# The causal mask of attention b added by VectorE inside the row-maximum operation, instead of by TensorE

## The reference

```
K = jnp.einsum('bpd,ihd->biph', x, W_K)
Q = jnp.einsum('bpd,ihd->biph', x, W_Q)
V = jnp.einsum('bpd,ihd->biph', x, W_V)
scores = jnp.einsum('biph,biqh->biqp', K, Q)
mask = jnp.tril(jnp.ones((q_len, q_len), dtype=bool))
scores = jnp.where(mask[None, None, :, :], scores, NEG_INF)
attn = jax.nn.softmax(scores / np.sqrt(d_head).astype(np.float32), axis=-1)
z = jnp.einsum('biph,biqp->biqh', V, attn)
z_flat = jnp.transpose(z, (0, 2, 1, 3)).reshape(b, q_len, -1)
out = jnp.einsum('bqf,df->bqd', z_flat, W_O)
```

## Time and profile before

| | |
|---|---|
| median of 3 executions | 586.08 us (585.6 to 588.6) |
| the profiled execution's own time | 586.4 us, of which the profile's span is 584.6 us |
| TensorE (matmul) busy | 461.3 us, 79% of the span |
| VectorE busy | 380.9 us, 65% |
| ScalarE busy | 225.5 us, 39% |
| GpSimd busy | 239.2 us, 41% |
| share of the chain that ended last | PE 64%, DVE 12%, POOL 9%, DMA 6% |
| row maxima (L1280), all instructions | 128, 62.4 us busy |

### The profile page before, as it was taken

How to read it: one execution, slowest core, us unless ns; L and a number is a source line. 1 busy time by engine, 2 the same in 40 slices (tenths; PEclk the granted TensorE clock), 3 DMA queues, 4 the chain that set the end, 5 groups by cost and what they waited for, 6 DMA issues and landing times.

```text
span 584.6 us, 10870 instructions
## 1 busy us (share of the span) xinstructions
PE 461.3 (79%) x3458; PEld 363.6 (62%) x3458; DVE 380.9 (65%) x1097; ACT 225.5 (39%) x815; POOL 239.2 (41%) x249
## 2 busy tenths in 40 slices
PE   2955694706997099999999999999999964609993
PEld 1422363606996067787877778787777854508993
DVE  6999986843665467767576765757676527825662
ACT  1600001402443046646355554645555333304441
POOL 6202784571544224434343343434334423562543
PEclk9967998556999599999999999999999987558998
DMA  8999500025472200000000000000000000126560
GB/s 293 413 421 422 213 1 1 28 105 167 106 226 72 72 2 2 1 2 1 0 0 0 0 0 0 0 0 0 0 0 0 1 2 1 55 93 185 156 196 20
DMA packets 22003, 47.57 MB, mean 81 GB/s; under 512 B 3248, under 2 KB 13622, under 8 KB 19536
## 3 DMA queue, kind: packets, MB, share of 16 engines
q1 hardware_dynamic: 18960, 40.79, 20.2%
q0 software_dynamic: 3008, 6.34, 3.1%
HBM read 23.88 MB, written 24.15 MB: 82 GB/s over the span
## 4 chain that ended last, share of the span: by engine, by line
PE 64%; DVE 12%; POOL 9%; DMA 6%; issue 5%; ACT 2%; SPq 0%; POOLq 0%; ACTq 0%; DVEq 0%
PE ps L836 10%; PE ps L865 8%; PE ps L904 8%; PE ps L891 7%; PE ps L791 6%; PE ps L853 5%; PE ps L804 5%; PE ps L843 5%; POOL sum L440 3%; DMA pv<-in_w 3%; PE ps L871 3%; POOL sorted_in L464 3%; PE ps L645 2%; POOL sum L444 2%; DVE prod L981 2%
## 5 line engine op out<-in xcount | busy, mean ns | idle before, releaser
L499 POOL TENSOR_TENSOR vT<-vT,prec 128x256 f32<-128x256 f32 (+1 forms) x128 | 103.0, 825 | 168.3 <-DVE prec L1288 168.3
L606 ACT ACTIVATE vT<-ps,nmax 128x128 f32<-128x128 f32 (+1 forms) x256 | 105.1, 435 | 26.1 <-DVE nmax L1280 26.1
L614 ACT COPY prod<-ps 128x384 f32<-128x384 f32 x96 | 42.9, 481 | 117.6 <-PE ps L891 114.2
L1280 DVE TENSOR_REDUCE nmax<-ps 128x2 f32<-128x256 f32 (+1 forms) x128 | 62.4, 550 | 33.9 <-PE ps L871 33.9
L836 PE MATMUL ps<-xnT,wb 128*128 128x256 f32 x256 | 67.0, 385 | 4.6 <-DVE xnT L1260 3.9
L891 PEld LDWEIGHTS ps<-cst,vT 128*128 128x128 f32 x384 | 44.7, 141 | 18.7 <-issue 15.8
L606 ACT ACTIVATION_READ_ACCUMULATOR vT<-ps,nmax 128x1 f32 x256 | 56.1, 219 | 0.0
L891 PE MATMUL ps<-cst,vT 128*128 128x128 f32 x384 | 52.5, 273 | 1.8 <-POOL vT L499 1.7
L904 PE MATMUL ps<-prod 128*64 128x256 f32 (+1 forms) x512 | 49.6, 336 | 3.0 <-ACT prod L614 2.1
L865 PE MATMUL ps<-qk 64*128 64x128 f32 (+1 forms) x512 | 51.0, 338 | 0.0
L836 PEld LDWEIGHTS ps<-xnT,wb 128*128 128x128 f32 x256 | 44.3, 193 | 10.5 <-DVE xnT L1260 4.3
(11 more groups left out here) (148 smaller groups left out, 832.4 us busy)
## 6 DMA issues: line engine op xcount, KB each, us to landing
sorted_in<-zero SPq DMA_DIRECT2D x1, 16512.0 KB, 58.6
pv<-in_w SPq DMA_DIRECT2D x30, 259.0 KB, 3.1
pv<-sorted_in SPq DMA_DIRECT2D x46, 129.0 KB, 2.6
wps<-in_w SPq DMA_DIRECT2D x1, 2072.0 KB, 9.2
w2s<-in_w SPq DMA_DIRECT2D x1, 2048.0 KB, 13.9
wb<-in_w_b SPq DMA_DIRECT2D x1, 1536.0 KB, 18.0
xres<-in_x SPq DMA_DIRECT2D x4, 256.0 KB, 4.0
xres<-after_ffn SPq DMA_DIRECT2D x4, 256.0 KB, 3.8
```

The costliest lines, as they stand in the source:

```text
L499: last = nc.gpsimd.tensor_tensor(px, px, view(prec, m_at(n, x) + t * 2, [[1, 2], [0, (t + 1) * P]]), ALU.mult)
L606: last = nc.scalar.activation(pb[:, o:o + (t + 1) * P], wide[:, c:c + (t + 1) * P], ACT.Exp, bias=nmax[:, m:m + 1], accum_out=psum[:, m:m ...
L614: nc.scalar.copy(pT[:, c:c + BLOCKS * P], bank[hh][:, 0:BLOCKS * P]).then_inc(b_pa, 1)
L1280: last = nc.vector.tensor_reduce(nmax[:, m:m + 2], view(wide, x * 1024 + t * P, [[512, 2], [1, (t + 1) * P]]), AX.X, ALU.max, negate=True)
```

## The change

The mask matmuls go, with their two bfloat16 tiles and the casts that filled them. `max_b` becomes eight tensor_tensor_reduce operations a step, one for each head and tile. Each reads the scores from PSUM and the mask from SBUF, writes minus their sum back over the scores in PSUM, and gives the minimum of what it wrote, which is minus the row maximum, through the accumulator. For tile 1 the mask row is 128 zero columns (new, at `C_OPEN` of the constants) followed by the causal block. The exponential takes scale -1. `b_s` is now raised once a step, after the scores of both pairs, and VectorE waits for it ahead of `invert(n, 1)`.

```
@@ -62,7 +62,7 @@
 SKIP = 4096.0
 
 
-C_ID, C_BEFORE, C_CAUSAL, C_FIRST, C_UPTO = 0, 128, 256, 384, 392
+C_ID, C_BEFORE, C_OPEN, C_CAUSAL, C_FIRST, C_UPTO = 0, 128, 256, 384, 512, 520
 C_SLOT = C_UPTO + NE * NE
 C_NEXT = C_SLOT + NDYN
 C_FULL = C_NEXT + NDYN
@@ -241,8 +241,6 @@
 
         wb = sb("wb", [P, 3 * HB * DHB])
         wob = sb("wob", [P, NPAIR * D])
-        id_bf = sb("id_bf", [P, P], BF16)
-        causal = sb("causal", [P, P], BF16)
         qk = sb("qk", [P, RING * 2 * L])
         nmax = sb("nmax", [P, 2 * 2 * 2 * T])
         psum = sb("psum", [P, 2 * 2 * 2 * T])
@@ -604,7 +602,7 @@
                         o, m = p_at(n, x, hh, t), m_at(n, x) + t * 2 + hh
                         c = (2 * x + hh) * 512 + t * P
                         last = nc.scalar.activation(pb[:, o:o + (t + 1) * P], wide[:, c:c + (t + 1) * P], ACT.Exp,
-                                                    bias=nmax[:, m:m + 1], accum_out=psum[:, m:m + 1])
+                                                    bias=nmax[:, m:m + 1], scale=-1.0, accum_out=psum[:, m:m + 1])
                 last.then_inc(b_e, 1)
 
             def copy_p(n, x, hh):
@@ -862,16 +860,11 @@
                     for hh in range(2):
                         rows = slice(hh * DHB, (hh + 1) * DHB)
                         c = (2 * x + hh) * 512 + t * P
-                        nc.tensor.matmul(wide[:, c:c + (t + 1) * P], qk[rows, r + t * P:r + (t + 1) * P],
-                                         qk[rows, r + L:r + L + (t + 1) * P],
-                                         start=t == 0, stop=False, skip_group_check=True)
-
-            def mask_b(x):
-                for hh in range(2):
-                    last = nc.tensor.matmul(view(wide, (2 * x + hh) * 512, [[2 * P, 2], [1, P]]), id_bf[:],
-                                            view(causal, 0, [[0, 2], [1, P]]), start=False, stop=True,
-                                            skip_group_check=True)
-                last.then_inc(b_s, 1)
+                        last = nc.tensor.matmul(wide[:, c:c + (t + 1) * P], qk[rows, r + t * P:r + (t + 1) * P],
+                                                qk[rows, r + L:r + L + (t + 1) * P],
+                                                start=t == 0, stop=t == T - 1, skip_group_check=True)
+                if x == 1:
+                    last.then_inc(b_s, 1)
 
             def turn_p(n, x):
                 pe.wait_ge(b_n, 2 * nth(n) + x + 1)
@@ -912,11 +905,8 @@
                 if ok(n1):
                     scores_b(n1, 0)
                     scores_b(n1, 1)
-                    mask_b(0)
                 if ok(n):
                     turn_p(n, 0)
-                if ok(n1):
-                    mask_b(1)
                 if ok(n2):
                     project_qk(n2, 0)
                 if some(bv) and j != 1 or some(b) and j == 1:
@@ -1045,9 +1035,7 @@
                 norm_a(u)
             dve.wait_ge(in_c, 16)
             nc.vector.tensor_copy(before[:], cst[:, C_BEFORE:C_BEFORE + P])
-            nc.vector.tensor_copy(id_bf[:], ident)
-            nc.vector.tensor_copy(region[:], cst[0:1, C_REGION:C_REGION + GT * NE])
-            nc.vector.tensor_copy(causal[:], cst[:, C_CAUSAL:C_CAUSAL + P]).then_inc(in_r, 1)
+            nc.vector.tensor_copy(region[:], cst[0:1, C_REGION:C_REGION + GT * NE]).then_inc(in_r, 1)
             for c in range(4):
                 products(0, c)
             products(1, 0)
@@ -1273,13 +1261,18 @@
                 dve.wait_ge(b_t, 4 * nth(n) + 4)
                 nc.vector.tensor_copy(pT[:, 2 * BLOCKS * P:3 * BLOCKS * P], bank[0][:, 0:BLOCKS * P]).then_inc(b_pd, 1)
 
+            def scored(n):
+                dve.wait_ge(b_s, nth(n) + 1)
+
             def max_b(n, x):
-                dve.wait_ge(b_s, 2 * nth(n) + x + 1)
-                for t in range(T):
-                    m = m_at(n, x) + t * 2
-                    last = nc.vector.tensor_reduce(nmax[:, m:m + 2],
-                                                   view(wide, x * 1024 + t * P, [[512, 2], [1, (t + 1) * P]]),
-                                                   AX.X, ALU.max, negate=True)
+
+                for hh in range(2):
+                    for t in range(T):
+                        m, c, open_at = m_at(n, x) + t * 2 + hh, (2 * x + hh) * 512 + t * P, C_CAUSAL - t * P
+                        s = wide[:, c:c + (t + 1) * P]
+                        last = nc.vector.tensor_tensor_reduce(out=s, in0=s, in1=cst[:, open_at:C_CAUSAL + P], scale=-1.0,
+                                                              scalar=-MASKED * 2, op0=ALU.add, op1=ALU.min,
+                                                              accum_out=nmax[:, m:m + 1])
                 last.then_inc(b_mx, 1)
 
             def invert(n, x):
@@ -1297,6 +1290,8 @@
                 bv = b + j // 2
                 if ok(at(b, j - 1)):
                     copy_z(at(b, j - 1))
+                if ok(n1):
+                    scored(n1)
                 if ok(n):
                     invert(n, 1)
                 if ok(n1):
```

## The result

Before 586.87 us (585.6 to 588.6, 4 executions), after 594.08 us (590.32 to 597.01, 4): ratio 1.0118, 95% interval 1.0071 to 1.0166, which is 6.9 us. A second set of executions gave 594.0 against 585.96, ratio 1.011 (1.0059 to 1.016). The direction was as forecast. The size was not: +20 us, to 606, was the forecast. The range from 594 to 630 holds the measured 594.08 by 0.1 us, and only because its lower end had been stretched to take in a part of rival (2).

A forecast was written before the change was run, and what follows sets the result against it. TensorE was taken to bound attention b, with VectorE almost on the path. Longer VectorE steps gave +18.7 us over eight batches; 18.7 - 0.5 + 1.4 + 0.2 = +19.8 on 586 made 606, range 594 to 630 (8 in 10).

The forecast's parts named there:

- rival (2): VectorE's new operations overlap more than reductions do, M from 2.3 to 2.65: 586 to 598 us, chance 0.11.
- What bounds the kernel before: Attention b: TensorE bounds, 7.55 us a step; VectorE, 67% busy, almost on the path; values could start 0.15 earlier.
- What is removed: TensorE's mask matmuls in attention b: 0.45 us a step over 32 steps, 14.4 us.
- What is added on VectorE: Four reductions become eight operations with accumulator reads at 0.08 us each; lower end 2.7 with reads at 0.055.
- M: Time from the first maximum operation's start to the last one's end in a VectorE step: 1.95 us before, 2.9 forecast.
- Where that lies: Operations lie between scores and the copy of p: step 5.20 + M = 8.1 us against 7.55 at j = 2, 3.
- Waits that move: GpSimd's division ends at 3.5 us instead of 2.6, ScalarE's first exponentials start at 3.2 instead of 3.0: no cost.
- the forecast's own case: M from 2.65 to 3.4 at full clock: 598 to 622 us, chance 0.60.
- Rivals (3): On VectorE each read waits for its operation and the next operation for the read: M 4.04, 642 us, chance 0.15.
- (4): The new VectorE operation runs at half rate: 1.6 us more in M, 4.5, and 657 us; chance 0.05.
- Rival (5): TensorE idles about 1 us a step and its mean clock falls to 0.86: 15 us more, 621; chance 0.04.
- four signs of being wrong: Pairs at 0.29 or less; TensorE gaps named GpSimd or ScalarE; clock below 0.95; values well before p's copy allows.

The follow-up runs named there:

- e8: Kernel before with one more 512-column reduction a step (0.60 us) on VectorE, behind the four: 598.01 us, ratio 1.0211.
- e3: Kernel before with one projection matmul of each step's first pair issued twice on TensorE (0.43 us a step more): 599.16 us, ratio 1.0187.
- e4: Changed kernel with attention b's causal mask left out and the four VectorE reductions of before: 577.15 us, ratio 0.9844.
- e5: Changed kernel with b_s raised for each pair again, so VectorE waits for each pair's scores apart: 575.62 us, ratio 0.9829.
- e9: Changed kernel with the eight operations lacking accumulator output and read (row maximum left out, bias 0): 580.38 us, ratio 0.9899.
- e7: Changed kernel with the causal mask left out and eight plain reductions a step, one per head and tile: 581.94 us, ratio 0.9926.
- e10: Changed kernel with the reciprocal of (n, 1) ahead of the wait for scores, which a 128x1 copy carries: 593.77 us, ratio 1.0134.
- e6: Kernel before with each pair's two mask matmuls right behind that pair's scores on TensorE: 598.41 us, ratio 1.019.

## Why the prediction was wrong in size, point by point

**What bounds the kernel before**: right in the main thing, that VectorE's stretch from the scores to the copy of p has almost no room (0.2 us, e8) though the engine is 67% busy. Wrong in the detail that the values could have started 0.15 earlier: TensorE sets the step with nothing to spare (e3).

**What is removed**: put at 0.45 us a step and 14.4 in all. It is 0.40 a step at j = 2 and 3, and e4 and e5 gave 11.9 and 12.0 over 31 steps: the turn of p takes 0.05 longer when it follows the scores directly. This did not touch the forecast, in which VectorE's stretch sets the step.

**What is added on VectorE**: this is the term that failed. M was put at 2.92, in the range 2.7 to 3.4. It is 2.61 (299.34 to 301.95, the last read's end), below the range. Two prices in it were too high. A read was given 0.08, nearer to the 0.09 of ScalarE's reads the earlier trace rows than to the 0.05 of the closest small operations on VectorE itself; it costs 0.048 (e9). Splitting four instructions into eight was given 0.33 and costs 0.22 (e7). Together 0.26 + 0.11 = 0.37 us a step, and 32 x 0.37 = 11.8 of the 12.9 us between the forecast +19.8 and the measured +6.9. The rest, 1 us, is less than the 1.4 that the first maxima and the last step were given; no run shows these two, nor the 0.2 us for the larger table of constants, apart from the scatter outside the steps.

The Trainium skill (Vector Engine (DVE) Microarchitecture Reference, section 5.2) has about 75 ns an instruction after overlap. An accumulator output with its read costs 48 ns here, so that the sum and the page agreed on 2.9 was no support for this term.

**Where that lies**: right (e7, e9). A step at j = 2 is 5.20 + M. In the terms of the prediction, M for the start of the copy of qk is 2.47 + 0.08 = 2.55, and 5.20 + 2.55 = 7.75 against 7.74; j = 1 7.85 against 7.82; j = 0 11.40 against 11.38. The waits are the two that were named.

**Waits that move**: right. GpSimd's division came later and nobody waited long for it (1.6 us in the whole stage; e10).

**Rivals**: the time fell into rival (2), M between 2.3 and 2.65, which had 0.11, just past the end of the forecast's own case. Rivals (3) and (4) are refuted by the timeline: operations and reads overlap, and 128 more columns cost 0.13 us. What the prediction quotes of the Trainium skill beside rival (3) (VectorE: DVE Perf Modes, section The DRAIN you can't avoid) is only half of it: the same paragraph goes on that an operation that is not held starts earlier, and the overlaps here don't contradict that. Rival (5) is refuted: the clock in the stage is 0.99. The forecast of TensorE's busy share, near 88%, was wrong at 96%, since its idle time a step came to some 0.4 us and not 1.

**The signs**: none of the four signs of being wrong showed. The pairs cost 0.31 us on average (2.47 / 8) against the 0.29 named, TensorE waited for VectorE's copies and 1.6 us in all for GpSimd, the clock was 0.99, and the values start 0.34 behind the copy of p. The signs were too coarse for this miss; what did show it was the batch, 34.66 us where 36.1 was forecast.

**The lower bound** was made from the closest pair of the earlier trace rows for the read alone, and kept the fixed cost of a reduction at 0.08 for each operation as if exact. By e7 that cost is 0.065 ((2.09 - 1.57) / 8, with 1536 columns at 1.02 ns). With it and reads at 0.048 the sum is 1.57 + 0.52 + 0.38 + 0.08 = 2.55, which is what was measured.

**What the prediction did not look for** is the joined wait. It costed `b_s` once a step as 0.10 us for the reciprocal, and took the start behind both pairs' scores as given. e5 shows that this one line decides the sign: starting each pair when its scores are there is worth 18 us, three times the loss. In the kernel before, the first pair's mask came behind the scores of both pairs, so VectorE could not start ahead of 1.94 anyway. With the masks gone the first pair's operations can start at 1.07 (e5), and the joined wait held them until 1.72.

## What to carry to other kernels

When work moves from a full engine to one that is two thirds busy, ask where in the cycle that engine's idle time lies: here it lay ahead of the end of the scores, and the new work behind them. Once a step is written as a sum along the second engine (5.20 + M), one number is left to get right, and its bounds must give each instruction its own range, the small ones too. And when a producer gets rid of a last stage, look again at when its consumers are told: a semaphore raised for both halves together hid the first half's readiness, and splitting it turned a loss of 1.2% into a gain of 1.7%.

## What the runs showed of the hardware

- A two-input VectorE operation that reads and writes PSUM in place (CUSTOM_DVE_ANT_0), without an accumulator output, runs at a plain reduction's pace: eight in 2.09 us, as eight reductions (e7, e9).
- With an accumulator output there is a read that lasts 0.14 us in the trace. It begins together with the next operation, and output and read add 0.048 us (2.47 against 2.09 for eight).
- A wait for the scores in a register operation ahead of the reciprocal lets it start 0.10 us later than one at the reciprocal itself (1.72 against 1.62 behind the scores' start, after).
- On TensorE, going from weights of 64 rows to weights of 128 and back once more in a step took 0.31 us (e6), more than the 0.23 us of two mask matmuls.
